# Self-attention and a Mamba-2 block in one kernel: the rows' maxima twelve steps ahead, their split, one convolution group and one residual moved in a hand-written step table

## The reference

```
q = wq x + bq ; k = wk x + bk         # 32 channels
attn = softmax(q^T k)                 # 4096 x 4096 per image
v = wv x + bv                         # 256 channels
x1 = gamma * (v attn^T) + x

u = layernorm over the 256 channels of x1, as 4096 tokens
z, xBC, dt = in_w u                   # 256, 512 and 4 columns
xBC = silu(causal 4-tap convolution along the tokens + conv_b)
state = state * exp(dt A) + dt x B ; y = state C + D x     # scan over the tokens, 4 heads of 64, state of 128
out = out_w (rmsnorm(y * silu(z)) * rms_w)
result = x1 + out * sigmoid(se2 relu(se1 mean(out)))
```

## Time and profile before

| | |
|---|---|
| median of 3 runs | 3107.33 us (3104.92 to 3109.52) |
| the profiled execution | 3107.73 us, its span 3105.6 us |
| granted TensorE clock over the span | 0.979 of full speed |
| DMA | 200.94 MB, mean 65 GB/s |

### The profile page before, as it was taken

One profiled execution on the slowest core, in us unless ns is written; L12 is line 12 of the kernel. 1 busy time (PEld: TensorE's weight loads), 2 busy tenths in 40 slices (PEclk: granted clock), 3 DMA queues, 4 the chain that ended last, 5 costly groups with the idle time before them and its releaser, 6 DMA issues. The chain is left out here.

```text
span 3105.6 us, 62448 instructions
## 1 busy us (share of the span) xinstructions
PE 2928.8 (94%) x20696; PEld 2256.1 (73%) x20696; DVE 2068.1 (67%) x3577; ACT 1926.2 (62%) x3806; POOL 1994.4 (64%) x3087
## 2 busy tenths in 40 slices
PE   6889999999999999999999999999999999999974
PEld 3767777777767777777777777777777777777752
DVE  5556666766766676666776667676766667776653
ACT  2556666666656666666665666666666666666642
POOL 2446665677665676666676666676777667777753
PEclk9999999999999999999999999999999999999985
DMA  3111111111311112122221122112121111112021
GB/s 121 53 32 43 47 58 58 32 49 55 98 71 65 58 65 89 68 78 75 91 84 37 65 72 87 65 68 89 40 90 36 50 64 45 68 50 70 35 96 68
DMA packets 102512, 200.94 MB, mean 65 GB/s; under 512 B 18768, under 2 KB 41936, under 8 KB 97808
## 3 DMA queue, kind: packets, MB, share of 16 engines
q1 hardware_dynamic: 98192, 195.08, 18.5%
q10 hardware_dynamic: 4000, 1.86, 0.2%
HBM read 131.21 MB, written 64.75 MB: 63 GB/s over the span
## 5 line engine op out<-in xcount | busy, mean ns | idle before, releaser
L727 POOL TENSOR_TENSOR p_lo<-p,p_hi 128x512 f16<-128x512 f32 x1024 | 1220.0, 1199 | 737.0 <-ACT p_hi L890 587.7
L883 ACT ACTIVATE p<-p_et 128x512 f32<-128x512 f32 x1024 | 614.6, 600 | 574.6 <-PE p_et L1141 511.1
L1159 PE MATMUL acc<-v_hi,p_hi 128*128 128x257 f16 x4096 | 954.5, 273 | 6.6 <-DVE work L1463 5.6
L1161 PE MATMUL acc<-v_lo,p_hi 128*128 128x256 f16 x4096 | 952.4, 273 | 0.0
L1419 DVE TENSOR_REDUCE maxes<-p_mx 128x1 f32<-128x1024 f32 x508 | 619.3, 1219 | 267.9 <-PE p_mx L1120 267.6
L890 ACT ACTIVATE p_hi<-p 128x512 f16<-128x512 f32 x1024 | 646.2, 631 | 8.3
L1167 PE MATMUL acc<-v_hi,p_lo 128*128 128x257 f16 x4096 | 622.8, 274 | 17.1 <-POOL p_lo L727 17.1
L1159 PEld LDWEIGHTS acc<-v_hi,p_hi 128*128 128x128 f16 x4096 | 403.6, 99 | 133.2 <-issue 71.8
L1161 PEld LDWEIGHTS acc<-v_lo,p_hi 128*128 128x128 f16 x4096 | 400.6, 98 | 103.3 <-issue 43.4
L1167 PEld LDWEIGHTS acc<-v_hi,p_lo 128*128 128x128 f16 x4096 | 399.9, 98 | 70.4 <-POOL p_lo L727 18.3
L1141 PE MATMUL p_et<-qs,kst 98*128 98x256 f16 x2048 | 393.1, 273 | 3.6 <-ACT p L883 2.9
(11 more groups left out here) (214 smaller groups left out, 4139.9 us busy)
## 6 DMA issues: line engine op xcount, KB each, us to landing
work<-rows_d SPq DMA_DIRECT2D x32, 1024.0 KB, 4.9
xin<-in_x_dram SPq DMA_DIRECT2D x48, 512.0 KB, 5.0
xr<-in_x_dram SPq DMA_DIRECT2D x32, 512.0 KB, 3.7
x_d<-x1c SPq DMA_DIRECT2D x31, 512.0 KB, 3.1
og_d<-og SPq DMA_DIRECT2D x29, 512.0 KB, 2.7
mix_x<-x_d SPq DMA_DIRECT2D x25, 512.0 KB, 4.7
mix_o<-og_d SPq DMA_DIRECT2D x24, 512.0 KB, 5.6
out_dram<-mix_o SPq DMA_DIRECT2D x24, 512.0 KB, 3.0
```

The source lines that it names most:

```text
L727: e.tensor_tensor(p_lo[:, n % RING, :], p32[:, n % P32S, :], p_hi[:, n % RING, :], ALU.subtract).then_inc(lo_pool, 1)
L883: e.activation(p32[:, n % P32S, :], p_et[:, :], ACT.Exp).then_inc(exp_done, 1)
L1159: e.matmul(acc[:, t, 0:C + 1], p_hi[:, r, at:at + P], v_hi[:, 2 * k + kk, 0:C + 1], start=(k == 0 and kk == 0), stop=False)
L1161: e.matmul(acc[:, t, 0:C], p_hi[:, r, at:at + P], v_lo[:, 2 * k + kk, :], start=False, stop=False, skip_group_check=True)
```

## The change

Five things move; no operation is added or removed.

```
-K_XBC = (11, 16, 20, 26)
+K_XBC = (11, 16, 21, 26)
-K_XT = (13, 19)
-K_XB = 4
+K_XT = (5, 19)
+K_XB = 2
...
-AHEAD = 10
+AHEAD = 12
...
-K_PARTS, K_MR, K_QR = STEPS - AHEAD, STEPS - AHEAD + 2, STEPS - AHEAD + 3
+K_PARTS, K_MR, K_QR = STEPS - AHEAD, STEPS - AHEAD + 3, STEPS - AHEAD + 4
...
-    early = {8: 0, 10: 1, 12: 2, 13: 3, 14: 4}
+    early = {8: 0, 9: 1, 10: 2, 12: 3, 13: 4, 14: 5}
```

## The result

The changed kernel takes 3125.29 us (median of 6 runs, 3119.84 to 3129.96) against 3107.02 us before (6 runs, 3104.92 to 3109.52): a ratio of 1.0058, 95% interval 1.0045 to 1.0071. It is slower by 18 us where I forecast 27 us less. The profiled execution of it took 3121.97 us, its span 3119.8 us, so the traces show 14.2 of the 18 us. In the following, "before" and "after" are the two kernels.

What follows compares the result with a forecast made beforehand. PE, busy 94% of the span, was taken as the bound, so only its waits could be gained: 54 us removed less 26.5 us added gives 27.5 us less, 3080 us from 3107.3, range 3064 to 3102.

Steps and rivals of the forecast that it cites:

- (h): Next image's input maximum at step 22 delays the product past step 26: 1 us lost, plus 1 us for plain slots.
- (f): Steps 20 to 23, six slots: second v waits for `v_low`, 8 us lost; fill at 25 waits for "mr", 2 us.
- slower rival: Steps 22 to 24: POOL blocks three small DVE instructions every slot, PE waits 2 us each; 3142 us, chance 0.07.
- (a): Step 24: the transpose's wait for the split on DVE goes, 24 times 1.2 us, 28 us gained.
- (b): Step 20: the third convolution group's wait for its bank goes with the move to 21, 19 us gained.
- (c): Step 13: "xT" no longer waits for the state fill of step 12 in three slots, 4.5 us gained.
- (d): Step 9: "uT" waits less for `query_rows`, now ahead of `mix` on DVE, 2.5 us gained.
- (e): Step 8: fill y waits for "mr", whose reader is `query_rows`, 1.9 us in five slots, 9.5 us lost.
- (g): Steps 4 and 20, three slots each: `mix` behind the split delays PE's fills at 6 and 26, 3 us lost.
- (i): Half 0: PE waits for the one bank pair at steps 9 and 10, 1.1 us each, 2 us lost.
- given back by the banks: Bank waits also in slots with seen slack, some 0.7 us in each of 31; about 3103 us, chance 0.09.
- More gained: Losses at fill y of step 8 and v of step 23 hidden by PE's other queued work; 3060 us, chance 0.10.

Runs made afterwards that it cites:

- e7: Before with only the maxima twelve steps ahead and the split at 4 and 20, transpose kept at 8 and 24: 3081.5 us, 0.9919.
- e5: After with POOL's remainder at steps 8, 9 and 10 of every half, from the second on, over one column only (work left out): 3079.42 us.
- e3: After with the transpose of the split back at steps 8 and 24 and the query rows at 9 and 25: 3088.73 us, 0.9947.
- e6: Before with only the residual at step 2 and the first half's fill "xT" at step 5: 3093.33 us, 0.9954.
- e2: After with the third convolution group back at step 20: 3103.49 us, 0.9987.
- e8: After with transpose at 8 and 24, query rows at 9 and 25, norm at 21, POOL's root kept at 24: 3048.79 us, 0.9816.
- e9: Before with only the third convolution group at step 21: 3116.9 us, 1.0031.
- e11: Before with only the maxima twelve steps ahead, the transpose at 7 and 23 and the query rows at 8 and 24: 3117.09 us, 1.0036.
- e10: After with the transpose at 8 and 24, the query rows at 9 and 25 and the third group at 20: 3068.89 us, 0.9878.

## Why the prediction was wrong

**The step that failed** is (h), with the last sentence of the part on the rule: "By my sum one is stretched now and then". The text counted one stretched instruction in a slot at most, and 1 us for all plain slots together. The trace has 988 ns in the middle for L1474 and 1037 for L1476, the first of them, of 32 slots (instead of 169 and 170):

```profile
L1474 DVE TENSOR_SCALAR rw<-rw x32: 170/988/1142, 317.1 to 3083.0; 128x4 int32<-128x4 int32 x32
```

So about 1.7 us more in most slots (L1474 took over 0.6 us in 29 of the 32, L1476 in 23). And the room was measured at the wrong reader. I followed the product to PE's fill at step 26 (slack 0.6 us) and never the tap to the tanh, behind which, in ACT's list, stand the copy and the exponential that PE's energies at 26 want. The price was 30.4 us at step 25 (32.8 less the 2.4 of (f) there) and 2.3 at 26, 32.7 us where the sum had 2. Put into the sum, it alone turns -27.5 into +3.2. The slower rival had the cause, POOL stretching the norm in every slot, but with the fill at 26 as its path, a size of 62 us and a chance of 0.07, taken from two slots of before in which the norm stood behind the split. Those durations did not carry over to an order without the split in front (e7 has them stretched with the group at 20 too). The text says itself that the norm no longer runs behind a split that has waited the lock out; it did not follow this into the sum: I should have priced "both stretched, every slot" as a bound of (h), as the rule I cited would have it. By that rule (the Trainium skill, SBUF — State Buffer, "SBUF: two separate sides"), of a GpSimd instruction and a VectorE instruction that uses the shared pair of ports, the one that starts first holds the pair to its end, and the other blocks. After and e5 agree with it: the median is 1037 ns beside full remainders of 1.16 us and 170 beside short ones, and in slot 7 of after L1476 ends at 787.11 where POOL's run ends at 787.09.

**The other terms**, predicted against measured by steps (after, slots 1 to 30):

| term | predicted | measured |
|---|---|---|
| (a) transpose | -28 | -27.6 (e7) |
| (b) third group's bank | -19 | -16.7 |
| (c) "xT" at 13 | -4.5 | -11.4 (5 and 13 together) |
| (d) "uT" at 9 | -2.5 | -1.6 (slots 12 and 20), step 9 in all -0.4 |
| (e) y at step 8 | +9.5 | +21.1 (7 and 8) |
| (f) v at 23, fill at 25 | +8, +2 | +12.9, +2.4 |
| (g) `mix` behind the split | +3 | not seen apart |
| (h) norm and product | +2 | +32.7 |
| (i) half 0 | +2 | +2.4 |
| not foreseen: v and z at 14 and 15 | 0 | +6.2 |
| not foreseen: step 16 | 0 | -4.1 |

(a) and (b) were right in mechanism and size. In (c) the mechanism held in three slots, but a constant wait of 0.23 us in every slot was taken for the normal case. (d) came in part: in slots 12 and 20 "uT" waits 0.18 us instead of 0.97, but there y has already held PE up by more; in slot 28 it waits 1.88 us for the state's reader, where it waited 1.78 for `query_rows`.

(e) had the right mechanism and the wrong count. Timeline of after in slot 12, step 8, to be set beside the earlier trace rows:

```profile
1214.69 0.38 PE L1141 MATMUL p_et<-qs,kst 98*128 98x256 f16 x2
...
1215.54 1.23 DVE L1419 TENSOR_REDUCE maxes<-p_mx 128x1 f32<-128x1024 f32 x1 [0.50 <-PE p_mx L1120]
...
1216.80 0.43 DVE L1436 CAST qs<-pl 2x256 f16<-2x256 f32 x1
...
1217.28 0.70 PE L1231 MATMUL pl<-S,xc 128*128 128x256 f32 x2 [1.78 <-DVE qs L1436]
```

y starts 2.59 us after the step instead of 0.65: 1.9 us late, as worked out. But there are eight such waits, not five. Besides slots 4, 9, 12, 17 and 20 they are in 10, 18 and 26, where a fill of the gate stands between the transpose and y and puts "mr" two before y. Timeline of after, slot 10, steps 7 and 8:

```profile
1018.80 0.27 PE L1128 MATMUL pl<-identh,mparts 128*2 128x128 f16 x2
1019.02 0.60 PE L1263 MATMUL pl<-hdn,se2T_sb 64*128 64x1 f32 x4
...
1023.00 0.43 DVE L1436 CAST qs<-pl 2x256 f16<-2x256 f32 x1
1023.48 0.70 PE L1231 MATMUL pl<-S,xc 128*128 128x256 f32 x2 [1.78 <-DVE qs L1436]
```

Steps 7 and 8 of these eight slots lose 16.6 us by the wait (2.14 us in the five, 1.96 in the three), and 7.2 us more in four of them at the lower clock (last section); the other slots give 2.7 back, as in e3. (f) was 1.9 us in five slots instead of 1.3, and 3.6 in slot 5, which has a spell of lower clock. With POOL's remainders short (e5) each of the six loses 0.96 us less, so half of it is again the norm's stretched instructions: slot 10 of after, steps 22 and 23, beside the earlier trace rows:

```profile
1071.61 0.38 PE L1141 MATMUL p_et<-qs,kst 98*128 98x256 f16 x2
...
1071.81 1.14 DVE L1474 TENSOR_SCALAR rw<-rw 128x4 int32<-128x4 int32 x1
...
1073.13 0.75 DVE L1413 SCALAR_TENSOR_TENSOR vst_lo<-pl,scs,vst_hi 128x512 f16<-128x512 f32 x1
...
1073.93 1.99 PE L1105 MATMUL pl<-wvT_sb,xin 128*128 128x256 f32 x8 [1.74 <-DVE vst_lo L1413]
```

The waits at 14 and 15 are a step I did not write down at all: "xT" leaves the list at 13, and v and z (L1204) get other predecessors. I had traced the new neighbours at 8 and at 23 and not at 14. They come with e6 too (+6.5), so they belong to "xT". What I had costed at nothing (the residual in step 2, the queries' load) shows in no step.

Of the rivals, "given back by the banks" (about 3103) was right that the banks take more, by other slots than it named: (e), (f) and steps 14 and 15 took 11.6 + 5.3 + 6.2 = 23.1 us more than forecast, 8.9 of them at the lower clock. That e2 took 3103.49 us is no proof of it: e2 has these losses and not that of step 25, but it also gives up the 16.7 us of (b) and has more of (c) than forecast, and that these come out near 3103 is chance. "More gained" fell: nothing hid (e) and (f).

## What to carry to other kernels

Where an engine's chain of short instructions changes its neighbours, take their durations from the order in which they will stand, and price the case in which each meets a long POOL instruction; measure the slack to every reader of the chain, and to what is queued behind that reader. A small instruction that leaves can matter as much as one that comes: here the split had shielded the norm behind it. When fills share two banks in turn, write down the new predecessor of every fill in every kind of slot, for the ones removed from the list as well as for those added. Moves that cost time together may be good one by one: here a table with "mr" at 8/24, the norm ahead of the group and its root left in place takes 3048.79 us from the same operations.

## What the runs showed of the hardware

A DVE instruction on 128 rows of four numbers took 170 ns, or, under POOL's remainders, about 1 us (medians of 988 and 1037 ns in after, 1158 in e8): in e5, where only POOL's remainders became short, the median went from 1037 back to 170 ns. Of a row of such instructions those that fall in POOL's run are long, and those behind it are short: the split and not the norm in before and e9, the norm in e7 and after.

Some of the loss ran at a lower clock. Windows of after (us from the span's start: length, busy us and instructions of PE, PEld, DVE, ACT and POOL, granted clock, DMA share, GB/s), the second in a spell that before doesn't have:

```profile
450.00:460.00 10.00, 9.96 (x70) 7.87 (x68) 5.78 (x8) 7.59 (x14) 9.04 (x10) 1.00 0.06 16
462.00:468.00 6.00, 6.00 (x26) 4.68 (x26) 0.76 (x3) 0.00 (x0) 1.45 (x3) 0.50 0.00 0
```

In these spells the granted clock is 0.50, the lower of its two levels (1.2 instead of 2.4 GHz). This one comes with the wait at y in slot 4: the matmuls of L1231 there take 1.19 us instead of 0.70, and step 8 takes 8.60 us, against 5.72 in slot 12 with the same wait. Shorter spells stand behind the wait at y in slots 10, 18 and 26 (1.4 to 1.5 us more each) and at (f) in slot 5 (1.7 us): 8.9 us of after's loss in the five, and they are part of the steps' sums above, (e) above all. In slots 1 to 30 before has three spells with 30.7 us at the half clock, all at the waits for POOL's remainder in slots 1, 9 and 17; after has eight with 51.2 us, e9 47.8, e11 51.2, and e6, e7, e8 and e10 23.9 us each. They stand where PE idled more, but not at every such place; what exactly starts one is not settled by these runs.
